# Graph attention over 8192 nodes: ScalarE copies the turned own rows, the indices stand in one list, and the pick comes ahead of decode, list and count

## The reference

```python
h = jnp.maximum(_layernorm(x, axis=-1), 0.0)
x = x + _L0_gnn_ref(h, adj, L0_gnn_W, L0_gnn_a)
h = jnp.maximum(_layernorm(x, axis=-1), 0.0)
x = x + _L1_gnn_ref(h, adj, L1_gnn_Wq, L1_gnn_bq, L1_gnn_Wk, L1_gnn_bk, L1_gnn_Wv, L1_gnn_bv)
```

## Time and profile before

| | |
|---|---|
| median of three runs | 1703.05 us |
| the profiled execution | 1698.98 us |
| its span, first to last instruction | 1697.2 us |
| busy in the span: TensorE, VectorE, ScalarE, GpSimd | 70%, 72%, 55%, 67% |
| mean granted TensorE clock | 0.705 |
| moved by the transfer engines | 368.10 MB, mean 217 GB/s |

### The profile page before, as it was taken

One profiled execution on the slowest core, in us unless ns is written; L12 is line 12 of the kernel. 1 busy time (PEld: TensorE's weight loads), 2 busy tenths in 40 slices (PEclk: granted clock), 3 DMA queues, 4 the chain that ended last, 5 costly groups with the idle time before them and its releaser, 6 DMA issues.

```text
span 1697.2 us, 23466 instructions
## 1 busy us (share of the span) xinstructions
PE 1195.3 (70%) x5503; PEld 944.0 (56%) x5554; DVE 1220.4 (72%) x6625; ACT 928.7 (55%) x1891; POOL 1131.2 (67%) x1206
## 2 busy tenths in 40 slices
PE   2667877877877778777765566766776676767676
PEld 1344555555555555555545456665766666666665
DVE  3567888888888888888888366656665665566565
ACT  2769888888878878888852222332233323332322
POOL 1237766766766666666666477777777777777773
PEclk9878777777777778777775566567566666566665
DMA  9869999999999999999922122222222222222221
GB/s 293 347 238 394 399 401 400 392 384 378 378 385 380 385 381 386 369 388 386 378 59 56 50 58 57 66 65 65 64 66 66 65 63 66 64 66 64 66 65 41
DMA packets 113049, 368.10 MB, mean 217 GB/s; under 512 B 33553, under 2 KB 58642, under 8 KB 80146
## 3 DMA queue, kind: packets, MB, share of 16 engines
q1 hardware_dynamic: 66242, 285.50, 43.6%
q0 software_dynamic: 38464, 81.08, 17.4%
q10 hardware_dynamic: 8208, 0.03, 0.3%
HBM read 353.80 MB, written 12.72 MB: 216 GB/s over the span
## 4 chain that ended last, share of the span: by engine, by line
POOL 33%; DVE 27%; PE 20%; issue 13%; ACT 4%; DMA 2%; SPq 1%; POOLq 0%; ACTq 0%; DVEq 0%
POOL arena L598 32%; PE psum L1443 6%; PE psum L1429 4%; PE psum L1415 4%; ACT arena L1175 3%; PE psum L1382 3%; DVE arena L754 2%; DVE arena L757 2%; DMA table<-arena 1%; DVE arena L880 1%; DVE arena L864 1%; DVE arena L875 1%; DVE arena L892 1%; DVE arena L889 1%; DVE arena L827 1%
## 5 line engine op out<-in xcount | busy, mean ns | idle before, releaser
L568 POOL DMA_INDIRECT arena<-table,arena x576 | 553.8, 961 | 260.2 <-issue 160.6
L598 POOL DMA_INDIRECT arena<-table,arena x576 | 549.0, 953 | 184.0 <-issue 174.9
L1175 ACT ACTIVATE arena<-arena 128x2048 bf16<-128x2048 int32 x256 | 484.8, 1894 | 26.0 <-DMA arena<-in_adj_dram 26.0
L1382 PE MATMUL psum<-arena 128*128 128x512 bf16 x973 | 283.7, 428 | 51.5 <-ACT arena L1175 46.8
L864 DVE SCALAR_TENSOR_TENSOR arena<-arena 128x131 f32<-128x131 f32 (+1 forms) x768 | 267.0, 348 | 15.1
L1429 PE MATMUL psum<-arena 128*128 128x131 f32 (+1 forms) x768 | 200.6, 433 | 103.8 <-ACT arena L1317 102.1
L1415 PE MATMUL psum<-arena 128*128 128x18 f32 x768 | 145.1, 322 | 166.1 <-DVE arena L827 165.7
L1415 PEld LDWEIGHTS psum<-arena 128*128 128x128 f32 x768 | 138.4, 265 | 185.0 <-DVE arena L827 184.7
L1429 PEld LDWEIGHTS psum<-arena 128*128 128x128 f32 x768 | 179.1, 329 | 107.5 <-issue 107.5
L1382 PEld LDWEIGHTS psum<-arena 128*128 128x128 bf16 x1024 | 110.0, 116 | 189.0 <-issue 67.4
L1422 PE MATMUL psum<-arena 128*128 128x1 f32 x768 | 134.7, 291 | 108.0 <-DVE arena L847 108.0
(11 more groups left out here) (205 smaller groups left out, 2089.3 us busy)
## 6 DMA issues: line engine op xcount, KB each, us to landing
arena<-in_adj_dram SPq DMA_DIRECT2D x256, 1024.0 KB, 12.2
arena<-table,arena POOLq DMA_INDIRECT x1152
table<-arena POOLq DMA_DIRECT2D x32, 132.0 KB, 4.5
table<-arena SPq DMA_DIRECT2D x16, 256.0 KB, 9.6
arena<-table SPq DMA_DIRECT2D x64, 64.0 KB, 1.9
out_dram<-arena SPq DMA_DIRECT2D x16, 256.0 KB, 2.4
arena<-in_x_dram SPq DMA_DIRECT2D x4, 0.5 KB, 12.2
arena<-in_L_gnn_W_dram SPq DMA_DIRECT2D x1, 64.0 KB
```

The lines of the kernel that those rows point to most:

```text
L568: pool.indirect_dma_start(Gt[:, v % GROUP, c + 1, :], None, table0, bass.IndirectOffsetOnAxis(idx_now[:, v % GROUP, c:c + 1], 0))\
L598: pool.indirect_dma_start(Gt[:, t % GROUP, c + 1, 0:D], None, table1, bass.IndirectOffsetOnAxis(idx_now[:, t % GROUP, c:c + 1], 0))\
L1175: nc.scalar.activation(mask[:, k, q * QUARTER:(q + 1) * QUARTER], adj_sb[:, k, q, :], ACT.Relu, accum_out=sum_all[:, bass.ds(tile, 1), q:q ...
L1382: nc.tensor.matmul(V[k], shifted[:, s, :], mask[:, k, s * 512:(s + 1) * 512], start=(s == 0), stop=False)
```

## The change

Three things change. The copy of the turned rows goes from VectorE to ScalarE, between its writing of the normalized rows and its third quarter; the turned rows then stand in the two banks of the sums, alternately, and no longer in the bank of the projections, so TensorE waits for other things. `idx_now` is gone: `pick` writes into `idx_all`, GpSimd reads its indices there in both phases, and `publish` and the second phase's wait go too. And `pick` stands ahead of `decode`, `list_tile` and `count` in VectorE's step.

```diff
-        self_turned_ps = bank(7)[:, 384:384 + P]
+        self_turned_ps = [bank(5 - k)[:, 256:256 + P] for k in range(2)]
...
-                                            bass.IndirectOffsetOnAxis(idx_now[:, v % GROUP, c:c + 1], 0))\
+                                            bass.IndirectOffsetOnAxis(idx_all[:, v, c:c + 1], 0))\
...
-                nc.vector.tensor_scalar(idx_now[:, b, :], dealt[:, b, LISTED:over + CHUNKS], 0.0, float(N), ALU.max, ALU.min)\
+                nc.vector.tensor_scalar(idx_all[:, v, :], dealt[:, b, LISTED:over + CHUNKS], 0.0, float(N), ALU.max, ALU.min)\
                   .then_inc(idx_done, 1)
-                dve.wait_ge(idx_done, v + 1)
-                nc.vector.tensor_copy(idx_all[:, at, :], idx_now[:, b:b + 1, :]).then_inc(pick_done, 1)
...
-                    if live(t, TURN):
-                        keep_self_turned(t - TURN)
...
+                    if live(t, TURN):
+                        o = t - TURN
+                        act.wait_ge(self_turned, o + 1)
+                        at_least(act, self_done, o)
+                        nc.scalar.activation(self_hT[:, :], self_turned_ps[o % 2], ACT.Identity).then_inc(self_hT_done, 1)
                     quarter(3)
...
-                        at_least(pe, chained, OWN * (o - 2) + 1)
-                        nc.tensor.transpose(self_turned_ps, Gt[:, o % GROUP, 0, 0:D], ident[:, :]).then_inc(self_turned, 1)
+                        at_least(pe, summed, o - 2)
+                        nc.tensor.transpose(self_turned_ps[o % 2], Gt[:, o % GROUP, 0, 0:D], ident[:, :]).then_inc(self_turned, 1)
...
                         pe.wait_ge(self_hT_done, o + 1)
+                        if o >= 1:
+                            pe.wait_ge(e_done, 3 * (o - 1) + 1)
+                        if o >= 2:
+                            pe.wait_ge(chained, OWN * (o - 2) + 1)
```

More of the change, by code:

```diff
@@ L127, in two_layer_graph_attention @@
         hot = place([GROUP, CHUNKS, OVER])
-        idx_now = place([GROUP, ROWS - 1], U32)
         owned_list = place([GROUP, CHUNKS, DEALT])
@@ L595, in _ @@
                     pool.wait_ge(summed, T + t - 3)
-                    pool.wait_ge(idx_done, T + t + 1)
                     for c in range(ROWS - 1):
                         pool.indirect_dma_start(Gt[:, t % GROUP, c + 1, 0:D], None, table1,
-                                                bass.IndirectOffsetOnAxis(idx_now[:, t % GROUP, c:c + 1], 0))\
+                                                bass.IndirectOffsetOnAxis(idx_all[:, t, c:c + 1], 0))\
                             .then_inc(rows_in[t % GROUP], 16)
@@ L788, in mark @@
                   .then_inc(mine_done, 1)
-            PICK_STEPS = 6
+            PICK_STEPS = 5
             def pick(v, b):
@@ L871, in add_self @@
                 nc.vector.tensor_scalar(acc_sb[:, k, 0:D + 2], self_ps[k], p10[:, k, 0:1], None, ALU.mult).then_inc(chained, 1)
-            def keep_self_turned(o):
-                dve.wait_ge(self_turned, o + 1)
-                nc.vector.tensor_copy(self_hT[:, :], self_turned_ps).then_inc(self_hT_done, 1)
             def total(tt, k, width):
@@ L968, in survey @@
                             keep_rows(UNITS - 1)
+                    if live(t, PICK):
+                        pick(v, v % GROUP)
                     if live(t, 1):
@@ L975, in survey @@
                             count(t - 2, (t - 2) % GROUP, pair)
-                    if live(t, PICK):
-                        pick(v, v % GROUP)
                     if live(t, DONE):
@@ L1095, in _ @@
             with dve.Else():
-                def publish(t, b):
-                    nc.vector.tensor_copy(idx_now[:, b:b + 1, :], idx_all[:, bass.ds(t, 1), :]).then_inc(idx_done, 1)
                 def prepare(t, b):
@@ L1136, in attend @@
                         back, m = (b - 3) % GROUP, (b - 3) % 2
-                        if live(t, -1):
-                            publish(t + 1, (b + 1) % GROUP)
                         if live(t, 1):
@@ L1160, in _ @@
                 dve.wait_ge(dve_consts, DVE_CONSTS + 3)
-                publish(0, 0)
                 unrolled(attend, G + 1)
```

## The result

The changed kernel took 1688.73 us (median of four runs, 1687.92 to 1689.55); the kernel before took 1703.14 us beside it (four runs, 1699.79 to 1706.76). The ratio is 0.9915 with a 95% interval of 0.9894 to 0.9936. So the change is worth 14.4 us by the medians, 11 to 18 by the interval, about half of the 27 us forecast. The profiled execution after has a span of 1687.2 us at a mean granted clock of 0.696.

What follows compares the result with a forecast made beforehand. First layer paced by VectorE waiting for TensorE, transfers next; second layer by GpSimd issuing gathers. 56 x 0.51 = 28.6, plus 4, less 5.6: 27 us, 1672, for the median 1676 us; range 1650 to 1697, 8 in 10.

Steps and rivals of the forecast that it cites:

- rival B: First layer: transfers bind already near today's pace, slowest engine 12.6 us per tile; 12 us gained, 1691 us; chance 0.2.
- three signs of being wrong: Changed profile: transfers under 385 GB/s with 12.0 us steps; landing times growing, steps over 12.6; or VectorE idle before pick.
- VectorE's copies: VectorE's first-layer step: turned-rows copy leaving saves 0.75 us, second index copy 0.21, together 0.96 us.
- TensorE's tail: First-layer steps without decode: projection L1473 leaves about 0.6 us to gain; mean gain 0.78 us, step 12.03 us.
- ScalarE takes the copy: ScalarE's first-layer step: copy of about 271 ns costs 0, paid for by VectorE's sum coming 0.78 us sooner.
- The transfers are the next limit: First layer's loop: transfers at 400 GB/s hold the step at 12.30 us, not 12.03; 0.51 us gained per step.
- Rival C: VectorE's early pick, first layer: waits for ScalarE's copy L1234; steps 0.3 us longer, 17 us, 1720 us; chance 0.07.
- floor of 12.30 us: First layer's transfers: least time per step at 400 GB/s, from 12.81 x 384 / 400.
- The 5.6 us taken off for unevenness: First layer's loop: 0.1 us per step lost because VectorE, TensorE and transfers stand within 0.3 us of each other.
- The pick: VectorE's step: moved early at the same VectorE time; indices ready about 4 us earlier, GpSimd's idle time falls.
- The end of the layer: First layer's last steps without adjacency: addition sooner, GpSimd's last tiles earlier; five steps of about 0.8 us, 4 us.
- The publish of the second layer: Start of the second layer: removing the publish and its wait is worth 0, bounds 0 and 0.3 us.

Runs made afterwards that it cites:

- lighter: Changed kernel, SyncE's loop written out, three quarters of the columns loaded in adjacency quarters without a diagonal block (output of another graph): 1645.26 us.
- copy_only: Kernel before with only ScalarE's copy of the turned rows; second index buffer, its copies and late pick stay: 1685.64 us.
- late_pick: Changed kernel with the pick back behind decode, list and count: 1688.02 us.
- lighter_fetch: lighter with the 25 SyncE increments behind each quarter's load as in fetch: 1645.85 us.
- fetch: Changed kernel, SyncE's loop written out, 25 increments of an unused semaphore behind each quarter's load, more instructions to fetch: 1697.07 us.

## Why the prediction was half right

The time lies in the stated 1650 to 1697 us, but just outside the 1666 to 1688 that the forecast had for itself and inside rival B's 1686 to 1698; the range held because it had room for B. Of the three signs of being wrong, B's came (landing times grew to 22.7 us with steps of 12.68), and C's in part (VectorE idles ahead of the pick, 18.6 us in 300 to 700 us).

*VectorE's copies* (-0.75 and -0.21, with TensorE's tail 0.78, 12.03 us per step): right. 12.04 us in steps 8 to 17, 11.97 over steps 8 to 64 of `lighter`. L1417 is late next, as said: 7.2 us before 31 additions. But nearly all of it is the copy of the turned rows. `copy_only`, which still has the index copy, takes 12.08 us in those nine steps, and `late_pick`, which differs from it only in having none, 12.10. So the 0.21 us for the index copy do not show; why is open.

*ScalarE takes the copy*: right. It took 257 ns against the 271 of the earlier trace rows, and the wait for the maxima that paid for it fell from 40.0 to 0.2 us.

*The transfers are the next limit*: right in its mechanism, and the step that failed in its size. I took a floor of 12.30 us from the rate of the stretch of 200 to 300 us, 400 GB/s, for all sixteen engines. But that is the rate of fifteen engines working off their queues ahead of one; it had fallen to 387 by 500 to 600 us. The loop's pace is the slowest engine's, 12.68 us. 45 steps x 0.38 = 17 us of the forecast are gone by that. The floor of 12.30 itself is close to the fit's 12.2 us without fetched instructions. The 5.6 us taken off for unevenness were no term of their own: `lighter`, where the transfers have room, runs at 11.97, no slower than the 12.03 of VectorE and TensorE. Rival B had both the reason (the slowest transfer engine, 12.6 us from the falling time to landing in the earlier trace rows) and the time, 1691. I had given it 0.2, because a figure for all engines was easier to read than the slope of a landing time.

*The pick*: "the same VectorE time" was right over the loop, wrong at its start. Rival C's wait came, 9.0 us in 100 to 180 us, and cost 3 to 4 us; that it costs nothing later, since VectorE has time while the adjacency is late, is likely (`late_pick` has steps of 12.69 without it, `lighter` shows none of it in 300 to 700 us) but was not tested by itself.

*The end of the layer*: 4 us forecast, 47.0 - 44.5 = 2.5 measured. No part has it alone: 46.8 with the early pick only, 46.4 with the copy only, 46.8 with all but the early pick. So the sooner addition, counted at 0.8 us a step, gave at most 0.6 in all five. L872 still waits for L1417 there, as two late steps (start, duration) show against the earlier trace rows:

```profile
889.53 1.51 PE L1417 MATMUL psum<-arena 128*128 128x131 f32 x6
891.08 0.30 DVE L872 TENSOR_TENSOR arena<-psum,arena 128x131 f32<-128x131 f32 x1 [0.82 <-PE psum L1417]
...
897.74 1.52 PE L1417 MATMUL psum<-arena 128*128 128x131 f32 x6
899.30 0.29 DVE L872 TENSOR_TENSOR arena<-psum,arena 128x131 f32<-128x131 f32 x1 [0.75 <-PE psum L1417]
```

*The publish of the second layer, 0*: right. The 9.0 us under its name in the earlier trace rows are 8.74 us under "issue" now, in front of the same gather.

The sum up to step 69: 13.7 us of pace, 2.5 at the end, less 4.0 at the start, 12.2 us (932.8 to 920.6). The two profiled spans differ by 10.0 us, mostly since the second layer's 576 gathers took 958 ns each after and 954 before; the medians differ by 14.4.

## What to carry to other kernels

Where transfers become the limit, look at the engine that lands last, not at the rate of all: here a time to landing that grew while GB/s looked healthy meant that one of sixteen engines was behind and that the rate would fall to its pace. Price a change by the limit behind it: here the freed 0.8 us per step met a transfer engine after nine steps. And before undoing other work, move transfers that don't belong in the loaded stretch out of it; here 1.3 per cent less load gave 9.5 us by the medians, 7 by the ratios.

## What the runs showed of the hardware

- Instructions are fetched by transfers that share the engines with the data. One 8 KB block goes with 0.5 to 0.6 us of delay on the loaded engine, by the fit, though its packet takes 0.31 to 0.33 us. The Trainium skill (Runtime: NRT & Kernel Launch, Instruction fetch mechanics) says that the cost of crossing into the next block is mostly hidden; `lighter_fetch` agrees, `fetch` does not. TensorE's 16 KB blocks, one packet of about 1.07 us, did not make their engine the last; why is open.
- The issue of a load can hold up SyncE. It took 0.35 us before at most, and up to 5.7 us after, in 500 to 800 us (min, median and max, ns). That full queues are the reason was not tested:

```profile
L456 SPq DMA_DIRECT2D arena<-in_adj_dram x95: 345/346/353, 500.2 to 799.7; - x95
```
```profile
L455 SPq DMA_DIRECT2D arena<-in_adj_dram x95: 345/346/5692, 499.5 to 798.8; - x95
```

- The Trainium skill (DMA: Bandwidth & Descriptors, Latency and other measured facts) knows two engines, 7 and 15, that are usually slower, and guesses at the rings of software descriptors. Here one engine is slower, and the delay per fetched block is enough to account for it: 12.2 + 0.4 us. No run shows its number.
